# Four of eight k-tiles of a 256-token matmul computed as seven block products instead of eight

## The reference

```python
x = x + (x @ W0.T + b0) + coeff[b] * (x @ (2 * mask[b] - 1))      # layer 0, mask is 1024 x 1024 for each batch
x = x + x @ w_eff.T                                               # layer 1: quantised weight plus low rank
x = x + (x @ W2.T + b2) + 2.0 * (x @ A2[i]) @ B2[i]               # layer 2, slot i by batch
x = x + (x @ B3[j].T) @ A3[j].T                                   # layer 3, slot j by batch
```

## Time and profile before

| | |
|---|---|
| median of three runs | 558.18 us (557.08 to 558.97) |
| the profiled execution | 557.65 us, its span 555.6 us |
| TensorE busy | 541.3 us, 97% of the span |
| VectorE, ScalarE, GpSimd busy | 398.2, 328.9, 157.8 us |
| DMA | 80.07 MB, mean 144 GB/s |
| granted TensorE clock | 1.0 |

### The profile page before, as it was taken

One profiled execution on the slowest core, in us unless ns is written; L12 is line 12 of the kernel. 1 busy time (PEld: TensorE's weight loads), 2 busy tenths in 40 slices (PEclk: granted clock), 3 DMA queues, 4 the chain that ended last, 5 costly groups with the idle time before them and its releaser, 6 DMA issues.

```text
span 555.6 us, 8876 instructions
## 1 busy us (share of the span) xinstructions
PE 541.3 (97%) x2892; PEld 464.6 (84%) x2892; DVE 398.2 (72%) x622; ACT 328.9 (59%) x622; POOL 157.8 (28%) x170
## 2 busy tenths in 40 slices
PE   5999999999999999999999999999999999999997
PEld 4988888888888788888888888888888888888886
DVE  5998898988956859666765875866687487586631
ACT  3877766776655846564564664656557466564620
POOL 2769778987714040021012002102100300210200
PEclk9999999999999999999999999999999999999999
DMA  8766042733577982574475366256447635634202
GB/s 230 246 88 143 21 145 62 248 97 113 120 192 231 314 204 97 170 186 69 149 221 113 132 187 156 63 170 197 76 151 226 114 119 163 174 73 151 76 0 76
DMA packets 138120, 80.07 MB, mean 144 GB/s; under 512 B 95664, under 2 KB 111024, under 8 KB 138096
## 3 DMA queue, kind: packets, MB, share of 16 engines
q1 hardware_dynamic: 137520, 78.71, 51.8%
q0 software_dynamic: 288, 1.05, 0.5%
q10 hardware_dynamic: 288, 0.01, 0.0%
HBM read 65.59 MB, written 14.16 MB: 144 GB/s over the span
## 4 chain that ended last, share of the span: by engine, by line
PE 84%; DVE 8%; ACT 4%; DMA 3%; issue 1%; POOL 0%; DVEq 0%; ACTq 0%; SPq 0%; POOLq 0%
PE bank L1432 19%; PE bank L1468 10%; PE bank L1469 10%; PE bank L1470 10%; PE bank L1439 10%; PE bank L1306 5%; PE bank L1308 5%; PE bank L1307 5%; PE bank L1478 3%; PE bank L1216 2%; PE bank L1485 1%; DVE merged_ring L1078 1%; DVE w_lo L984 1%; DMA mask_ring<-in_mask_Bx4096x_ik 1%; ACT bank L574 1%; PE bank L1230 1%
## 5 line engine op out<-in xcount | busy, mean ns | idle before, releaser
L1432 PE MATMUL bank<-x_t_pair,m_hi 128*128 128x512 f32 x512 | 128.4, 393 | 1.8 <-ACT m_hi L740 1.6
L740 ACT CAST m_hi<-merged_ring 128x512 fp32r<-128x512 f32 x128 | 73.0, 618 | 66.1 <-PE bank L1439 34.1
L1432 PEld LDWEIGHTS bank<-x_t_pair,m_hi 128*128 128x128 f32 x512 | 92.5, 189 | 19.5 <-ACT m_hi L740 2.6
L1084 DVE TENSOR_TENSOR m_lo<-merged_ring,m_hi 128x512 fp32r<-128x512 f32 x128 | 82.4, 689 | 30.7 <-ACT m_hi L740 30.6
L1468 PE MATMUL bank<-P_hi,x_t_pair 128*128 128x512 f32 x256 | 99.7, 389 | 0.0
L1469 PE MATMUL bank<-P_lo,x_t_pair 128*128 128x512 f32 x256 | 99.7, 389 | 0.0
L1470 PE MATMUL bank<-P_hi,x_t_pair 128*128 128x512 f32 x256 | 99.6, 389 | 0.0
L530 POOL TENSOR_TENSOR x_t_pair<-x_sum,x_t_pair 128x256 fp32r<-128x256 f32 x32 | 24.8, 801 | 260.5 <-ACT x_t_pair L781 260.5
L1078 DVE TENSOR_TENSOR merged_ring<-merged_ring,w_t 128x1024 f32<-128x1024 f32 x64 | 78.3, 1234 | 21.6 <-ACT merged_ring L730 20.6
L730 ACT ACTIVATE merged_ring<-mask_ring,batch_now 128x1024 f32<-128x1024 int32 x64 | 77.9, 1241 | 23.1 <-DMA mask_ring<-in_mask_Bx4096x_ik 22.3
L1439 PEld LDWEIGHTS bank<-x_t_pair,m_lo 128*128 128x128 f32 x512 | 69.9, 190 | 5.0
(11 more groups left out here) (152 smaller groups left out, 869.6 us busy)
## 6 DMA issues: line engine op xcount, KB each, us to landing
mask_ring<-in_mask_Bx4096x_ik SPq DMA_DIRECT2D x64, 512.0 KB, 4.5
out<-out_staged SPq DMA_DIRECT2D x32, 256.0 KB, 2.1
w_nat<-in_L_cond_W SPq DMA_DIRECT2D x14, 512.0 KB, 5.1
x_t_squares<-in_x SPq DMA_DIRECT2D x56, 128.0 KB, 2.7
w_raw<-in_L_cond_weight SPq DMA_DIRECT2D x16, 256.0 KB, 4.5
g_batch<-g_dram SPq DMA_DIRECT2D x32, 128.0 KB, 4.5
w0t_dram<-w_out SPq DMA_DIRECT2D x14, 256.0 KB, 2.7
w_t<-w0t_dram SPq DMA_DIRECT2D x6, 512.0 KB, 5.2
```

The costliest lines, as they stand in the source:

```text
L740: nc.scalar.copy(Mh[:, n % MR], ring_f[:, k % MR, h * HALF:(h + 1) * HALF]).then_inc(s["h_set"], 1)
L1084: nc.vector.tensor_tensor(Ml[:, n % MR], ring_f[:, k % MR, h * HALF:(h + 1) * HALF], Mh[:, n % MR].bitcast(F32), ALU.subtract).then_inc(s[ ...
L1432: mm(bank[L0_BANK[HT * h + j]][:, :], Mh[:, n % MR, j * P:(j + 1) * P], xThl[:, :, :, k + i, :], start=(k + i == 0), stop=False, skip_grou ...
```

## The change

Of main's eight k-tiles, tiles 0 to 3 are taken as a 2 x 2 block product in batches 2 to 7: tokens in halves 0 and 1, k-tiles in pairs X = (0, 1) and Y = (2, 3), columns in halves. The Winograd form needs seven block products, with four sums S1 to S4 of x1's blocks (for each batch) and four sums T1 to T4 of P's blocks (once). Tiles 4 to 7 stay as they were. In detail:

- TensorE: a block product is 2 k-tiles by 3 matmuls. Seven of them replace eight. Four are done ahead of `rank`, three as part of the outputs. The outputs' order is (0,0), (1,0), (0,1), (1,1); the fourth has only k-tiles 4 to 7.
- VectorE, in each of batches 2 to 7: four sums of x1 (`a_sums`) ahead of `m_lo` 7, their low parts (`a_lo`) behind it, and four sums out of PSUM (`c11_seen`, `c22_sums`) ahead of the turning of x; `out_add` 2 stands ahead of `m_lo` 1. ScalarE: four high parts (`a_hi`). GpSimd: `v_bias`, `p_bias`.
- VectorE in batches 0 and 1: nine operations of 128 x 1024 for T1 to T4 and four for their low parts; ScalarE four for the high parts. T takes the place of `w0_t` in SBUF.
- Since `w0_t` is gone, W0's rows come from `w0t_dram` in every batch from 1 on: 8 loads of 512 KB into two landing slots. The load for tile j waits for `merged` j-2. SyncE issues them between the masks.
- The output stores are issued by GpSimd, the last two by SyncE.

```diff
...
+    Th = at("t_hi", [P, 4, 2, HALF], F32R, reg_z1 + 8 * KB)
+    Tl = at("t_lo", [P, 4, 2, HALF], F32R, reg_z1 + 24 * KB)
+    Tw = at("t_scratch", [P, 4, 2, HALF], F32, reg_z1 + 8 * KB)
+    Ts = at("t_sum", [P, 4, 2, HALF], F32, reg_z1 + 24 * KB)
+    Ss = at("s_sum", [P, KT, D], F32, reg_p + 32 * KB)
+    land = at("w0_landing", [P, 2, D], F32, reg_z3)
...
-        MAIN_BANK = [3, 6, 7, 4]
-        RANK_BANK = 5
+        OUT = [(0, 0), (1, 0), (0, 1), (1, 1)]
+        MAIN_BANK = [3, 5, 7, 4]
+        P6_BANK = 6
+        RANK_BANK = 0
...
+            def load_w0(b, j):
+
+                sp.wait_ge(s["v_set"], KT * b + j - 1)
+                sp.dma_start(land[:, j % 2].rearrange("p (i n) -> p i n", i=2),
+                             w0t_dram[part_rows(j), :, part_cols(j)].rearrange("k p n -> p k n")).then_inc(w0_land[j % 2], 16)
+
+            def next_mask(b, k):
+                done = 2 * KT * b + 2 * k + 2
+                if k < MR:
+                    sp.wait_ge(s["m_ready"], done)
+                    load_mask(b, k + MR)
                 else:
-                    sp.wait_ge(s["out_done"], 4 * b)
+                    sp.wait_ge(s["m_ready"], done)
+                    load_mask(b + 1, k - MR)
...
+            def load_next(b, last):
                 if not last:
-                    for k in range(MR):
-                        sp.wait_ge(s["m_ready"], 2 * KT * b + 2 * (k + MR) + 2)
-                        load_mask(b + 1, k)
+                    for k in range(MR, KT):
+                        next_mask(b, k)
+                        if k < MR + 2:
+                            load_w0(b + 1, k - MR)
 
                     sp.wait_ge(s["m_used"], 2 * KT * (b + 1))
                     load_x(b + 1)
...
+            def batch(b, last=False):
+                load_w0(b, 2)
+                load_w0(b, 3)
+                next_mask(b, 0)
+                next_mask(b, 1)
+                load_w0(b, 4)
+                load_w0(b, 5)
+                load_w0(b, 6)
+                load_w0(b, 7)
+                next_mask(b, 2)
+                next_mask(b, 3)
+                sp.wait_ge(s["out_done"], 4 * b)
+                load_tables(b)
+                load_next(b, last)
...
+            def store(b, i):
+                t, h = OUT[i]
+                pool.wait_ge(s["out_added"], 4 * b + i + 1)
+                dst = out_rows[b, t, h] if isinstance(b, int) else out_rows[bass.ds(b, 1), t, h].rearrange("b p n -> (b p) n")
+                nc.gpsimd.dma_start(dst, staged[:, i % 2]).then_inc(out_stored[i % 2], 16)
...
+            with pool.Fori(3, NB) as b:
+                pool.wait_ge(s["u_done"], b)
+                c_copies(b)
+                v_bias(b - 1)
+                store(b - 1, 0)
+                p_bias(b - 1)
+                for i in range(1, 4):
+                    store(b - 1, i)
+                x1_lo(b)
...
+            def a_hi(b):
+                act.wait_ge(s["a_summed"], 4 * (b - 1))
+                for i in range(4):
+                    nc.scalar.copy(Ph[:, 0:2, a_cols(i)], Ss[:, 0:2, a_cols(i)]).then_inc(s["a_hi"], 1)
...
+                    dve.wait_ge(w0_land[j % 2], 64 * (b - 1) + 16 * (j // 2 + 1))
+                    row = land[:, j % 2].rearrange("p (i n) -> p i n", i=2)
...
+            def a_sums(b):
+                dve.wait_ge(s["x1_sum"], KT * b + HT)
+                t0, t1 = slice(0, P), slice(P, T)
+                nc.vector.tensor_tensor(Ss[:, X, a_cols(S1)], x1s[:, X, t1], x1s[:, Y, t1], ALU.add).then_inc(s["a_summed"], 1)
+                nc.vector.tensor_tensor(Ss[:, X, a_cols(S3)], x1s[:, X, t0], x1s[:, X, t1], ALU.subtract).then_inc(s["a_summed"], 1)
+                dve.wait_ge(s["a_summed"], 4 * (b - 1) - 3)
+                nc.vector.tensor_tensor(Ss[:, X, a_cols(S2)], Ss[:, X, a_cols(S1)], x1s[:, X, t0], ALU.subtract).then_inc(s["a_summed"], 1)
+                dve.wait_ge(s["a_summed"], 4 * (b - 1) - 1)
+                nc.vector.tensor_tensor(Ss[:, X, a_cols(S4)], x1s[:, Y, t0], Ss[:, X, a_cols(S2)], ALU.subtract).then_inc(s["a_summed"], 1)
+
+            def a_lo(b):
+                for i in range(4):
+                    dve.wait_ge(s["a_hi"], 4 * (b - 1) - 3 + i)
+                    nc.vector.tensor_tensor(Pl[:, 0:2, a_cols(i)], Ss[:, 0:2, a_cols(i)], Ph[:, 0:2, a_cols(i)].bitcast(F32),
...
+            def c11_seen(b):
+
+                dve.wait_ge(s["prod_done"], 4 * (b - 1) - 3)
+                nc.vector.tensor_tensor(c_sum[:, :], bank[MAIN_BANK[0]][:, :], b2all[:, 0:HALF], ALU.add).then_inc(s["c11_seen"], 1)
+                dve.wait_ge(s["prod_done"], 4 * (b - 1) - 2)
+                dve.wait_ge(s["c11_seen"], b - 1)
+                nc.vector.tensor_tensor(c_sum[:, :], c_sum[:, :], bank[P6_BANK][:, :], ALU.add).then_inc(s["c11_c6"], 1)
+
+            def c22_sums(b):
+
+                dve.wait_ge(s["prod_done"], 4 * (b - 1))
+                dve.wait_ge(s["c11_c6"], b - 1)
+                nc.vector.tensor_tensor(vsum[:, :], c_sum[:, :], bank[MAIN_BANK[1]][:, :], ALU.add).then_inc(s["v1_set"], 1)
+                dve.wait_ge(s["v1_set"], b - 1)
+                nc.vector.tensor_tensor(vsum[:, :], vsum[:, :], bank[MAIN_BANK[2]][:, :], ALU.add).then_inc(s["v2_set"], 1)
...
                 if not first:
                     merged(b, 0, first)
                     x_lo(b)
-                    for h in range(2):
-                        out_add(b - 1, 0, h, second)
+                    for i in range(2):
+                        out_add(b - 1, i, old, second)
                     merged(b, 1, first)
-                    for k in range(2):
-                        m_lo(b, k)
+                    m_lo(b, 0)
+                    out_add(b - 1, 2, old)
+                    m_lo(b, 1)
+                    if second:
+                        t1_sum()
                     merged(b, 2, first)
                     merged(b, 3, first)
-                    out_add(b - 1, 1, 0)
+                    out_add(b - 1, 3, old)
+                    if second:
+                        t2_part()
                     merged(b, MR, first)
-                    out_add(b - 1, 1, 1)
                     merged(b, MR + 1, first)
...
+            def batch(b):
+                layer0(b)
+                for kk in range(2):
+                    pe.wait_ge(s["x1_ready0"], HT * b + kk + 1)
+                    ins = product(bank[MAIN_BANK[0]][:, :], x1_of(kk, 0), p_of(kk, 0), start=(kk == 0), stop=(kk == 1))
+                ins.then_inc(s["prod_done"], 1)
+                pe.wait_ge(s["t_ready"], 4)
+                for o, i, j in ((P6_BANK, S2, T2), (MAIN_BANK[2], S1, T1), (MAIN_BANK[1], S3, T3)):
+                    pe.wait_ge(s["a_ready"], 4 * (b - 1) - 3 + i)
+                    for kk in range(2):
+                        ins = product(bank[o][:, :], sum_of(i, kk), t_of(j, kk), start=(kk == 0), stop=(kk == 1))
+                    ins.then_inc(s["prod_done"], 1)
+                rank(b)
+
+                pe.wait_ge(s["c11_seen"], b - 1)
+                for kk in range(2):
+                    product(bank[MAIN_BANK[0]][:, :], x1_of(2 + kk, 0), p_of(2 + kk, 0))
+                main(b, 0, range(HT, KT))
+                close(b, 0)
+
+                pe.wait_ge(s["v1_set"], b - 1)
+                for kk in range(2):
+                    product(bank[MAIN_BANK[1]][:, :], x1_of(2 + kk, 1), t_of(T4, kk))
+                main(b, 1, range(HT, KT))
+                close(b, 1)
+
+                pe.wait_ge(s["v2_set"], b - 1)
+                pe.wait_ge(s["a_ready"], 4 * (b - 1))
+                for kk in range(2):
+                    product(bank[MAIN_BANK[2]][:, :], sum_of(S4, kk), p_of(2 + kk, 1))
+                main(b, 2, range(HT, KT))
+                close(b, 2)
+                main(b, 3, range(HT, KT), True)
+                close(b, 3)
...
```

249 lines of the change are left out of this document (187 added, 62 removed).

## The result

The changed kernel took 596.04 us (median of 4 runs, 592.91 to 599.66), the kernel before, on the same chip, 558.26. The ratio is 1.068, 95% interval 1.062 to 1.075: slower by 38 us, where I had forecast 7. The range ended at 575.

What follows compares the result with a forecast made beforehand. TensorE's list was taken as the bound. Stalls of 2.2 us at five turns, plus 2.1 and 2.4, make 15.5; less 8.2 for saved matmuls, +7.3 us on 557.65, so 565.0 us; range 552 to 575.

Steps and rivals of the forecast that it cites:

- Main costs nothing: Main part, from layer0's end: u, sums and closes come in time, cost nothing, with 2.0 us of slack as cover.
- The new order at the turn: VectorE at the next batch's start: out_add 2 ahead of m_lo 1, m_lo 1 done at 22.25, merged 3 at 24.6 us.
- What does a 512 KB load take?: W0 and mask loads at the turn: old-trace landings, 0.57 us per further load; 5.35 us for tile 5's row.
- Stall one: layer0, pair 2's low matmuls: TensorE waits 1.3 us (0 to 2.5) because merged 5 waits for W0's tile 5 row.
- The traffic rival: Turns between batches: traffic is the bound, stalls of 4.1 us a turn, +18 us, 576 us; chance 0.15.
- Rival GpSimd: GpSimd and VectorE hold each other up around p_bias, out_add 2 comes 0.4 to 1.3 us later, 569 us; chance 0.1.
- Stall two: layer0, pair 7's high matmuls: TensorE waits 0.9 us (0.4 to 1.6) a turn for the chain from tile 6's mask.
- the 1.8 us that I made of it: The two stalls' loads: up to 1.8 us later each by the skill's latency under load, some 18 us; not summed.

Runs made afterwards that it cites:

- experiment 3: Changed kernel with W0's loads, same size and places, sent to a DRAM scratch and nobody waiting for them (W0 left out of the result): 590.75 us.
- experiment 1: Changed kernel without the repeated W0 loads from tile 2 of batch 1 on (W0 left out of the result): 557.16 us.
- experiment 11: Changed kernel plus eight throwaway matmuls in layer0 of batches 2 to 7, ahead of the wait for tile 4's high parts: 595.36 us.
- experiment 9: Version of experiment 8 plus four unread 512 KB loads a batch into a DRAM scratch, spread out: 571.68 us, ratio 1.022.
- experiment 8: Change with seven products for two k-tiles, half of W0 kept in SBUF, the rest loaded off the turn, SyncE stores, old out_add order: 556.76 us, ratio 0.9987.
- experiment 2: Changed kernel, all W0 waits kept, each load after the first two cut from 512 to 64 KB (most of W0 left out): 563.96 us.
- experiment 10: Version of experiment 8 plus four unread 512 KB loads a batch, all directly behind the turn's two masks: 580.88 us, ratio 1.040.
- experiment 5: Whole changed kernel with all output stores issued by SyncE instead of GpSimd: 595.29 us.

## Why the prediction was wrong

- **Main costs nothing: right.** Closes, sums, `rank` and the next `layer0` came within 0.1 us of the worked-out times; no wait stands there.
- **The new order at the turn: right** to 0.2 us, down to `merged` 3's end at 24.7 (24.6). The waits are in `layer0`, as said, and the one ahead of pair 2's low matmuls hangs on W0's row of tile 5, as said. But TensorE also waits ahead of pair 2's high matmuls (2.5 us in the turn shown), for `m_hi` 2 behind `signs` 5 and the mask of tile 5. This path is in no term. With the landing that I took for a second mask it would have been just in time (22.25 + 4.7 + 1.24 + 0.6 = 28.8, wanted at 28.7); with 6.9 it is late. And the mask of tile 6 stops TensorE at `m_hi` 5, right behind `signs` 6, in three of the turns, where I had looked at pair 7 alone.
- **"What does a 512 KB load take?": this step failed.** I took 5.35 us for tile 5's row (bounds 3.8 and 6.5) and 4.6 for tile 6's mask, both counted from the instruction that frees the slot. In the turn shown they took 8.0 and 6.2, so the turn comes to 2.2 + 2.7 + 1.6 = 6.5 by the prediction's own sum; the seven turns lost 6.5 on the mean, this one 7.3. The error is in the form of the term: a landing read in a batch that moves 145 GB/s was kept for a turn in which the DMAs move 250 to 284, and only "0.57 for each further load in the row" was added. The trace of before had the landing under traffic too, inside. Of the 512 KB rows of W0 there, the three asked for by 175 us landed in 3.7, 4.3 and 4.4 us. The next three, asked for from 175.5 to 180, when the DMAs became full, took 6.0, 8.3 and 8.0, and the two masks between them (175.94 and 179.06) 7.6 and 7.1. The kernel before, stretches from 174 us on, and the load of 176.49:

```profile
174.00:177.00 3.00, 3.00 (x20) 2.66 (x19) 3.00 (x4) 0.85 (x2) 2.37 (x3) 1.00 0.40 70
177.00:180.00 3.00, 2.85 (x17) 2.30 (x16) 2.92 (x5) 2.29 (x3) 0.53 (x1) 1.00 1.01 368
180.00:183.00 3.00, 2.94 (x17) 2.40 (x17) 3.00 (x5) 2.80 (x6) 0.00 (x0) 1.00 0.94 330
...
w_t<-w0t_dram SPq DMA_DIRECT2D x1, 512.0 KB, 8.3
```

- **A sum of bytes** would have shown most of it, and was never made. From the first mask's issue (430.8) two masks, two rows of W0 and two stores are asked for, 2.6 MB; with what was still on its way the DMAs moved 3.1 MB until tile 5's row was there (443.1). At the 284 GB/s shown above that is 11 us, so until 441.8, or 6.7 us for tile 5's row. The last 1.3 us of its 8.0 are not explained: the DMAs were nearly idle then.
- **Stall one, VectorE waiting for W0's row, as the main term: not needed.** With nobody waiting for W0 (experiment 3), a loss of 33.6 us stays. In the turn shown it set the start of pair 2's low matmuls (4.1 us late), but 2.6 of that would have come by the mask of tile 5 alone. The masks, which pass through the same DMAs, are a path of their own, from `signs` to `m_hi`.
- **The traffic rival (0.15, 576 us) was the right one,** and its "landings of 6.5 and 5.2 us or more" was still too mild; its evidence against ("most of the masks' landings stay near 4.5") was read from the kernel before, whose traffic is not the change's. The Trainium skill, in "DMA: Bandwidth & Descriptors", section "Latency and other measured facts", has the latency rise with load. No run here shows that latency by itself; landings 2.4 to 2.7 us later than I took for tile 5's mask and row, and 1.6 for tile 6's mask, agree with its direction, and the first two exceed the 1.8 us that I made of it, some 18 us in all, and left out of the sum.
- **Rival GpSimd: small.** `m_lo` takes 753 ns in the mean for 689, and GpSimd's x1 parts 968 for 801, but 751 and 967 in experiment 1 as well, which isn't slower than the kernel before.
- **Stall two without the traffic: near.** Predicted 0.9 a turn; experiment 1 lost 1.2 a turn in all, against the 1.36 saved.
- **The clock** was in no term. It fell to 1.2 GHz four times. The rows bound its share by 10.2 us of the 39.6; the fall in the turn shown cost nothing by its own rows (pair 7 above), and experiment 11 got nothing back for half of them.
- **What stays open.** The wait time that the trace lists for TensorE (31 us) less the matmuls saved (8.2) and with the clock's 10.2 makes 33, and the spans differ by 39.6. The other 6 us are no waits: TensorE's busy time rose from 541.3 to 549.7 although 8.2 of matmuls are gone, which is 16.6 us of slower matmuls, against 10.2 by the clock. How much the clock costs by itself was bounded, not measured. Nobody tried the masks ahead of W0's rows in SyncE's list. Batch 0's 2.1 us are in no term and weren't looked into. Reads of W0 without the scratch's writes weren't tried away from the turn, so the 13 us of experiment 9 may overstate what the change's reads would cost there.

## What to carry to other kernels

Saving TensorE work by giving up SBUF room moves the bill to the DMAs: sum the bytes that are asked for in each few microseconds of the new schedule, with those still on their way, and divide by the rate at which a full stretch of a trace runs, before taking any landing time from the old trace. Take the result as the least that the last load needs: tile 5's row took 1.3 us more. A mean of 185 GB/s says little when a turn asks for 2.6 MB in 6 us. Then follow every load to TensorE by each engine that waits for it, the ones with slack in the old trace too: the mask of tile 5 had slack, and became the first wait. And see where the saved time would show: here the masks' slots set the turn, and six matmuls less a batch bought 0.6 us even with W0 for nothing.

## What the runs showed of the hardware

- Landing of 512 KB loads moves with the traffic around them: mask median 4.5 us at a mean of 144 GB/s, 4.9 without the W0 loads (147), 5.9 to 6.2 at 185 to 187, and 6.0 to 8.0 us for the four loads read at the turn. The mean alone doesn't set it: 4.6 us at 171 GB/s in experiment 8, 5.7 at 152 in experiment 2 with its 64 KB loads, 5.5 at 189 in experiment 10.
- In stretches of 2 or 3 us with the DMAs' share at 0.9 or more they moved from 172 (507 to 509 us of the change) to 382 GB/s (experiment 9).
- The granted clock fell from 2.4 to 1.2 GHz in four places of the change and stayed there for 3 to 7 us, each time in or right behind a wait of TensorE: of 3.18 us (ended at 287.03), 1.82 (349.58), 2.49 (441.68) and 2.77 (506.65), while five waits of 1.5 to 1.9 elsewhere had none.
- A store issued by GpSimd landed in 4.0 us where SyncE's landed in 2.6 (experiment 5, where the stores also go out at other times); without W0's loads it was 2.3 and 2.1. Under experiment 9's loads SyncE's took 4.5.
